# A three-layer interaction network in split precision: one 400-column matmul per chunk becomes two of 200

## The reference

```python
# x: (512, 39, 32); W0: (39*39, 200), W1 and W2: (100*39, 200)
for i in range(3):
    z = einsum('bmd,bnd->bmnd', x, hidden).reshape(B, -1, D)   # hidden = x for layer 0
    cur = relu(einsum('bcd,co->bod', z, W[i]) + b[i][None, :, None])
    if i != 2:
        hidden, direct = cur[:, :100, :], cur[:, 100:, :]
    else:
        direct = cur
    finals.append(direct)
out = concatenate(finals, axis=1).sum(axis=-1)                # (512, 400)
```

## Time and profile before

| | before |
|---|---|
| median of 3 runs | 2921.2 us (2920.04 to 2921.68) |
| the profiled execution's own time | 2919.57 us |
| its span, first to last instruction | 2917.8 us |
| mean granted clock of TensorE | 0.990 |
| busy share PE / PEld / DVE / ACT | 97% / 91% / 91% / 64% |

### The profile page before, as it was taken

How to read it: one execution, slowest core, us unless ns; L and a number is a source line. 1 busy time by engine, 2 the same in 40 slices (tenths; PEclk the granted TensorE clock), 3 DMA queues, 4 the chain that set the end, 5 groups by cost and what they waited for, 6 DMA issues and landing times.

```text
span 2917.8 us, 58694 instructions
## 1 busy us (share of the span) xinstructions
PE 2820.6 (97%) x18688; PEld 2666.4 (91%) x18688; DVE 2668.5 (91%) x2706; ACT 1873.7 (64%) x3850; POOL 1.1 (0%) x11
## 2 busy tenths in 40 slices
PE   1699999999999999999999999999999999999998
PEld 1699999999999999999999999999999999999998
DVE  3799999999999999999999999999999999999997
ACT  2466666666666666666666666666666666666665
POOL 0000000000000000000000000000000000000000
PEclk8899999999999999999999999999999999999999
DMA  8344444344444344344344344344444434444441
GB/s 193 84 130 107 107 128 110 106 127 113 104 125 117 104 124 118 104 120 121 104 118 124 104 117 125 104 112 129 104 109 128 108 107 127 111 106 126 113 106 53
DMA packets 256151, 333.83 MB, mean 114 GB/s; under 512 B 61346, under 2 KB 190990, under 8 KB 256014
## 3 DMA queue, kind: packets, MB, share of 16 engines
q1 hardware_dynamic: 256138, 333.67, 43.9%
HBM read 332.73 MB, written 8.37 MB: 117 GB/s over the span
## 4 chain that ended last, share of the span: by engine, by line
PE 95%; DMA 2%; DVE 1%; SPq 1%; ACT 1%; issue 0%; DVEq 0%; ACTq 0%
PE acc L589 62%; PE acc L590 28%; PE summed L608 4%; PE turned L601 1%; DMA xb<-x_by_unit 0%; DMA xb<-in_L_rec_b_dram 0%; DVE z_low L346 0%; DMA w_rows_again<-in_L_rec_W_dram 0%; DMA xb<-in_L_rec_W_dram 0%; DVE z L342 0%; DVE w_split L319 0%; DMA out_dram<-o_row 0%; ACT w_split L487 0%; ACT z_high L454 0%; SPq L194 0%
## 5 line engine op out<-in xcount | busy, mean ns | idle before, releaser
L589 PE MATMUL acc<-w_split,z_high 128*128 128x400 f32 (+1 forms) x8832 | 2672.9, 368 | 77.5 <-DVE z_low L346 71.6
L590 PE MATMUL acc<-w_split,z_low 128*128 128x200 f32 (+1 forms) x8832 | 2255.7, 255 | 0.0
L589 PEld LDWEIGHTS acc<-w_split,z_high 128*128 128x128 f32 (+1 forms) x8832 | 1661.5, 188 | 166.9 <-issue 159.3
L454 ACT ACTIVATE z_high<-z 128x1024 fp32r<-128x1024 f32 (+2 forms) x1152 | 1179.3, 1024 | 814.9 <-PE acc L590 737.5
L590 PEld LDWEIGHTS acc<-w_split,z_low 128*128 128x128 f32 (+1 forms) x8832 | 1690.9, 191 | 0.0
L346 DVE TENSOR_TENSOR z_low<-z,z_high 128x1024 fp32r<-128x1024 f32 (+2 forms) x1152 | 1353.4, 1175 | 129.3 <-ACT z_high L454 129.2
L342 DVE TENSOR_TENSOR z<-hid,xb 128x1024 f32<-128x1024 f32 (+1 forms) x1024 | 1213.8, 1185 | 59.7 <-DMA xb<-x_by_unit 50.9
L475 ACT ACTIVATE hid<-turned 96x512 f32<-96x512 f32 x256 | 149.1, 582 | 132.2 <-PE turned L601 132.2
L478 ACT ACTIVATE hid<-turned 32x128 f32<-32x128 f32 x768 | 204.6, 266 | 8.9
L608 PE MATMUL summed<-s,group_b 128*4 128x100 f32 (+1 forms) x768 | 150.1, 277 | 1.4 <-ACT s L470 1.4
L351 DVE TENSOR_TENSOR s<-acc,half 128x200 f32<-128x200 f32 x384 | 137.8, 359 | 10.5 <-ACT half L459 10.5
(11 more groups left out here) (20 smaller groups left out, 13.5 us busy)
## 6 DMA issues: line engine op xcount, KB each, us to landing
xb<-x_by_unit SPq DMA_DIRECT2D x384, 384.0 KB, 4.8
x_right<-x_by_unit SPq DMA_DIRECT2D x384, 136.5 KB
xb<-x_by_unit SPq DMA_DIRECT2D x384, 128.0 KB, 5.7
xb<-x_by_unit SPq DMA_DIRECT2D x128, 336.0 KB
xb<-x_by_unit SPq DMA_DIRECT2D x128, 84.0 KB
x_left<-x_by_unit SPq DMA_DIRECT2D x384, 19.5 KB
out_dram<-o_row SPq DMA_DIRECT2D x256, 1.6 KB
xb<-in_L_rec_W_dram SPq DMA_DIRECT2D x6, 600.0 KB, 9.2
```

The costliest lines, as they stand in the source:

```text
L454: nc.scalar.activation(z_high[slot][0:rows, 0:n * T], z[slot][0:rows, 0:n * T], ACT.Copy).then_inc(high, 1)
L589: nc.tensor.matmul(a[:, 0:2 * O], z_high[slot][0:rows, tok], w, start=(c == 0), stop=False, skip_group_check=True)
L590: last = nc.tensor.matmul(a[:, 0:O], z_low[slot][0:rows, tok], w[:, 0:O], start=False, stop=(c == chunks - 1), skip_group_check=True)
```

## The change

A chunk is three matmuls of 200 columns, all into the accumulator's columns 0 to 199: z_high with the high weights, z_high with the low weights, z_low with the high weights. The accumulator's second half isn't used. `half`, `second_half`, `sums`, `dup` and `relu` are gone, with their semaphores; ACT's new `outputs`, at the places of `second_half`, reads the accumulator directly: for layers 0 and 1 a copy of the 100 factors to s, the repeated tail, and the relu of the direct part; for layer 2 one relu of 200 columns. `acc_free` waits for these on ACT.

```diff
-                    nc.tensor.matmul(a[:, 0:2 * O], z_high[slot][0:rows, tok], w, start=(c == 0), stop=False, skip_group_check=True)
+                    nc.tensor.matmul(a[:, 0:O], z_high[slot][0:rows, tok], w[:, 0:O], start=(c == 0), stop=False, skip_group_check=True)
+                    nc.tensor.matmul(a[:, 0:O], z_high[slot][0:rows, tok], w[:, O:2 * O], start=False, stop=False, skip_group_check=True)
                     last = nc.tensor.matmul(a[:, 0:O], z_low[slot][0:rows, tok], w[:, 0:O], start=False, stop=(c == chunks - 1),
                                             skip_group_check=True)
...
-            def sums(l, u):
-                dve.wait_ge(half_in[l], u + 1)
-                nc.vector.tensor_tensor(s[l][:, :, 0:HID], acc[l][:, 0:O].rearrange("p (h o) -> p h o", o=HID), half[l][:, :, :], ALU.add)\
-                  .then_inc(s_in[l], 1)
...
-            def second_half(l, u, last):
+            def outputs(l, u, last):
 
                 act.wait_ge(freed, RING + last + 1)
-                nc.scalar.activation(half[l][:, :, :], acc[l][:, O:2 * O].rearrange("p (h o) -> p h o", o=HID), ACT.Copy)\
-                  .then_inc(half_in[l], 1)
...
+                if l < 2:
+                    nc.scalar.activation(s[l][:, 0, 0:HID], acc[l][:, 0:HID], ACT.Copy)
+                    nc.scalar.activation(s[l][:, 0, HID:HID + TAIL_ROWS - TAIL].rearrange("p (j q) -> p j q", q=TAIL),
+                                         acc[l][:, MAIN:HID].unsqueeze(1).to_broadcast([P, TAIL_M - 1, TAIL]), ACT.Copy)\
+                      .then_inc(factors_in[l], 1)
+                    nc.scalar.activation(s[l][:, 1, 0:HID], acc[l][:, HID:O], ACT.Relu).then_inc(direct_in[l], 1)
+                else:
+                    nc.scalar.activation(s[l][:, :, :].rearrange("p h o -> p (h o)"), acc[l][:, 0:O], ACT.Relu).then_inc(direct_in[l], 1)
...
             def acc_free(l, u):
-                pe.wait_ge(s_in[l], u)
+
+                if l < 2:
+                    pe.wait_ge(factors_in[l], u)
+                pe.wait_ge(direct_in[l], u)
```

More of the change, by code:

```diff
@@ L93, in cin_kernel @@
         s = {0: sb("s0", [P, 2, P]), 1: sb("s1", [P, 2, P]), 2: sb("s2", [P, 2, HID])}
-        half = {l: sb(f"half{l}", [P, 2, HID]) for l in range(3)}
         ident = sb("ident", [P, P])
@@ L123, in cin_kernel @@
         freed = sem("freed")
[L124 to L127, removed]
+        factors_in = [sem(f"factors_in{l}") for l in range(2)]
+        direct_in = [sem(f"direct_in{l}") for l in range(3)]
         turned_in = [sem(f"turned_in{l}") for l in range(2)]
@@ L377, in _ @@
                     lows(1, 1, L0_ROWS, L0_CHUNKS)
-                    sums(0, 0)
-                if k == 3:
-                    sums(0, 1)
             dve.wait_ge(w_low_done, 1 + 2 * GROUPS)
@@ L392, in _, with period @@
             lows(at + 4, slot_of(at + 4), L0_ROWS, L0_CHUNKS)
-            sums(1, 0)
-            sums(0, 2)
-            def period(n, par, base, sl, layer0=True, sum2=True, last_low=True):
+            def period(n, par, base, sl, layer0=True, last_low=True):
                 def slot(p):
@@ L409, in period @@
                 lows(base + 2, slot(2), P, group_chunks(2))
-                if sum2:
-                    sums(2, n - 2)
                 q = 4
@@ L425, in period @@
                 lows(base + q + 1, slot(q + 1), P, group_chunks(1))
-                sums(1, n)
                 product12(2, n - 1, 1 - par, 3, base + q + 3, slot(q + 3))
                 lows(base + q + 2, slot(q + 2), P, group_chunks(2))
-                if layer0:
-                    sums(0, n + 2)
-            period(1, 1, first(1), first(1) % RING, sum2=False, last_low=False)
+            period(1, 1, first(1), first(1) % RING, last_low=False)
             with dve.Fori(0, (UNITS - 4) // 2) as i:
@@ L440, in _ @@
             product12(2, UNITS - 1, 1, 0, at, slot_of(at))
-            sums(2, UNITS - 2)
             for g in range(1, GROUPS):
@@ L445, in _ @@
             lows(at + 3, slot_of(at + 3), P, group_chunks(3))
-            sums(2, UNITS - 1)
         @block.scalar
@@ L497, in _ @@
                     highs(1, 1, L0_ROWS, L0_CHUNKS)
[L498 to L501, removed]
+                    outputs(0, 0, 0)
                 if k == 3:
@@ L504, in _ @@
                     results(0, 0)
[L505 to L508, removed]
+                    outputs(0, 1, 1)
                 if k == 7:
@@ L516, in _ @@
             highs(at + GROUPS, slot_of(at + GROUPS), L0_ROWS, L0_CHUNKS)
[L517 to L520, removed]
+            outputs(1, 0, at + 3)
+            outputs(0, 2, at + 4)
             def period(n, par, base, sl, layer0=True, before0=True, before2=True):
@@ L527, in period @@
                 highs(base, slot(0), P, group_chunks(0))
-                if before0:
-                    dup(0, n + 1)
-                    relu(0, n + 1)
                 highs(base + 1, slot(1), P, group_chunks(1))
@@ L534, in period @@
                 if before2:
-                    second_half(2, n - 2, base - 1)
+                    outputs(2, n - 2, base - 1)
                 results(1, n - 1)
@@ L543, in period @@
                     q = 5
-                if before2:
-                    relu(2, n - 2)
                 if before0:
@@ L549, in period @@
                 highs(base + q + 1, slot(q + 1), P, group_chunks(1))
-                second_half(1, n, base + 3)
+                outputs(1, n, base + 3)
                 highs(base + q + 2, slot(q + 2), P, group_chunks(2))
                 if layer0:
-                    second_half(0, n + 2, base + 4)
+                    outputs(0, n + 2, base + 4)
                 if before2:
@@ L556, in period @@
                 highs(base + q + 3, slot(q + 3), P, group_chunks(3))
-                dup(1, n)
-                relu(1, n)
             period(1, 1, first(1), first(1) % RING, before2=False)
@@ L567, in _ @@
             hidden(1, UNITS - 1, 1)
-            second_half(2, UNITS - 2, at - 1)
+            outputs(2, UNITS - 2, at - 1)
             for g in range(GROUPS):
@@ L571, in _ @@
             results(1, UNITS - 1)
-            relu(2, UNITS - 2)
             results(2, UNITS - 2)
-            second_half(2, UNITS - 1, at + 3)
-            relu(2, UNITS - 1)
+            outputs(2, UNITS - 1, at + 3)
             results(2, UNITS - 1)
@@ L594, in acc_free @@
             def acc_free(l, u):
-                pe.wait_ge(s_in[l], u)
+                if l < 2:
+                    pe.wait_ge(factors_in[l], u)
+                pe.wait_ge(direct_in[l], u)
             def transpose(l, u):
-                pe.wait_ge(tail_dup[l], u + 1)
+                pe.wait_ge(factors_in[l], u + 1)
                 if not (isinstance(u, int) and u == 0):
@@ L603, in sum_over_d @@
             def sum_over_d(l, u):
-                pe.wait_ge(relu_done[l], u + 1)
+                pe.wait_ge(direct_in[l], u + 1)
                 if not (isinstance(u, int) and u == 0):
```

## The result

The changed kernel takes 3285.72 us (median of 4 runs, 3284.47 to 3286.97) against 2921.44 for the kernel before (2920.04 to 2922.42): 1.1247 times the time before, 95% interval 1.1228 to 1.1267, or 364 us more. The forecast was 3200, in a range of 3180 to 3290.

The account below looks back on a forecast made before the run. PE's pace after about 125 us of start bounds the kernel: 8832 chunks, each 0.0316 us longer, add 279 us to 2919.6, giving 3199; the median's 1.6 us more makes 3200 us, range 3180 to 3290.

Parts of the forecast that it names:

- What bounds the kernel: Whole kernel: about 125 us of start, then PE's pace; 1 ns per chunk is worth 8.8 us.
- Step (1): z_high matmul split in two: three load steps per chunk, 0.325 us against 0.2933, +279 us (bounds +258, +367).
- Step (2): Sums over d and transposes between groups: 1.72 us per unit remain; taken as 0, at most -10 us.
- Step (3): Copy to half and addition gone, ACT reads acc: all beside PE work, worth 0 in the steady part.
- (5): Kernel's end: about 0.7 us saved, about 1 us lost in the first chunks at lower clock; they cancel.
- Step (4): Order on ACT: a z_high conversion later by at most about 0.5 us; price 0, without cover 190 us.
- the cover: PE's two groups of 8 chunks (2.3 us each) outlast a conversion (1.0) plus a subtraction (1.2), hiding ACT's delay.
- the other signs: Profile after: 26496 loads, starts 0.11 us apart, chunk 0.325, PEld near 100%, no PE waits after 125 us, DVE 82%.
- A: Chunk matmuls: load isn't the limit, 200-column matmuls follow at 0.0933 us; chunk 0.280, about 2802 us; chance 0.06.
- B: Second z_high matmul needs no second load: chunk 0.295 us, 2920 to 2935 us; chance 0.06.
- C: PE's granted clock falls: at 1.2 GHz a chunk takes 0.63 us, time above 5500 us; chance 0.02.

Follow-up runs that it names:

- the uneven split: Kernel before with the 400-column z_high matmul split into 280 and 120 columns, copy and addition kept: 3448.48 us (ratio 1.1809).
- 64-token run: Changed kernel with the middle matmul of each chunk on 64 of 128 tokens: 3110.10 us; with the z_low matmul on 64 too: 2947.41 us.
- The runs with one part alone: Kernel before with only the z_high matmul split: 3289.36 us; changed kernel with the 400-column matmul kept, only outputs from ACT: 2916.47 us.

## Why the prediction was right, and where its size was off

**What bounds the kernel** held. The loss is PE's pace in the steady part, and from 200 to 2400 us no matmul of the changed kernel waits for data.

**Step (1), three loads, each the limit,** is the cause, and is shown from both sides: shortening the load shortens the step (3286 to 3110 to 2947), shortening the stream doesn't (19066 against 19061 matmuls), and the uneven split cost the 160 us that the sum of maxima gives. Its size was off. I took 0.1083 per step and named 0.1116 as the upper bound; measured is 0.1118 on the eleven chunks shown, and 0.1115 to 0.1117 as the mean of all such steps from 200 to 2400 us. A step of 0.112 or more was my own sign that the forecast is wrong at its upper end, and the steps stand right there. The time is in the range, with 4 us to spare, because the range was drawn from that bound and not from the value that I took. Averaged over all chunks of that stretch that follow each other directly, a chunk went from 0.2937 to 0.3346 us, 0.0409 more where I had 0.0316: 8832 x 0.0093 = 82 us, nearly all of the distance from 3200 to 3286.

The sentence that failed is "the z_low load follows a load-bound z_high matmul with no such extra". In the kernel before there are 0.0033 us from the z_low matmul's recorded start to the z_high load, and 0.1083 from there to the next load; I counted the second part alone. The 64-token run has both kinds of step side by side: 0.111 up to its short load, where the step ahead is set by a load too, and 0.108 where the step ahead is set by the stream. The uneven split has the same two values, 0.111 behind a load-bound step and 0.108 behind the one of 280 columns. So 0.108 is the price of a load step behind a stream-bound one, and between load-bound ones it is 0.003 to 0.0035 more. That this is the same 0.0033, moved, fits the sum but isn't shown. The full price could be read in the earlier trace rows by starting from a matmul whose start its stream had set: from the z_low matmul at 1004.12 to the second load behind it at 1004.24, 0.1116 on the mean of the twelve.

**Step (2), sums and transposes:** with the mean chunk, a unit has 21.96 - 69 x 0.2937 = 1.70 us beside its chunks before and 24.81 - 69 x 0.3346 = 1.72 after. The 0 that I took was right; the up to 10 us of hidden load time didn't come. (The 0.3355 of the eleven chunks shown would give 1.66, but 0.01 us of resolution over eleven chunks is 0.06 in a unit.)

**Step (3) and (5), copy, addition and end:** taken at 0, with 0.7 us saved at the end against 1 us lost in the first chunks. The runs with one part alone say 4 us for all that isn't the split. No run tells the 1 us of the first chunks apart. At the end the rows after show one relu between the last two sums:

```profile
3280.19 0.09 PEld L571 LDWEIGHTS summed<-s,group_b 128*4 128x4 f32 x2
...
3280.96 0.31 ACT L446 ACTIVATE s<-acc 128x200 f32<-128x200 f32 x1
3281.32 0.09 PEld L571 LDWEIGHTS summed<-s,group_b 128*4 128x4 f32 x2 [1.04 <-ACT s L446]
```

From sum to sum 1.13 us instead of 1.93: 0.8 us, near the expected 0.7.

**Step (4), ACT's order:** the row of matmuls has no wait for L434 or L343 from 200 to 2400 us. The row of loads has one:

```profile
PEld acc L548 <- DVE z_low L343: 45.8, 177, 0.3
```

These are the gaps around sums, which before were put down to issue (69.3 us, 301 times). They have hardly grown: a sum among chunks adds 0.534 us to the step there, and 0.528 before. So the cover held. DVE's share is the forecast 82%, but of a longer unit: 20.3 us of 24.8, where I had 19.8 of 24.1. Of the other signs, PEld near 100% didn't come: it is busy 2109 of 2200 us, 96%, since the gaps around the sums remain.

**Rivals.** A (load not the limit) is refuted by the 64-token runs and by the step itself. The prediction set beside it a formula from the Trainium skill ("TensorE: Matmul & The Clock Gate", "Back-to-back issue gap"). That section gives the formula for an isolated matmul, and says that in a stream of loads and matmuls both set the spacing, with which these runs agree (0.1115 per pair, not 0.0858). B (a second load saved) didn't happen: there are 8832 loads for the second matmul, and the order of the three makes no difference. The Trainium skill ("TensorE: Matmul & The Clock Gate", "Step-by-step: what each phase is for") is right that load and matmul are separate, but in this program each fp32r matmul brings its own load, here as before. C (the clock) did not come in the changed kernel, but it was nearer than the 0.02 suggest: with 100 columns less per chunk the same kernel ran at the lower level from start to end.

## What to carry to other kernels

Price a matmul as the longer of its stream and of the weight load that must hide behind it, and add these up one by one; splitting a wide matmul adds no columns and still costs a load step wherever the pieces are narrower than the load (here below about 240 columns, an estimate: the 0.185 us of 400 columns are 0.4625 ns per column, and 240 of them make 0.111 us). Take the step in the profile around a whole cycle, and ask of each step what set the one ahead of it, since a load step cost 0.108 behind a stream and 0.1115 behind another load. The busy share doesn't tell: it stays at 97% either way. Save engine work beside the bound last; here it was worth at most 4 us against 364.

## What was not expected of the hardware

A step set by a 128x128 fp32r load took 0.108 to 0.112 us at the full clock and 0.213 at the lower one, and a load of 64 columns brought its step down to 0.095, about the 0.093 of a 200-column stream. In two of these runs streaming less cost much more than it could have saved. With 560 instead of 600 columns per chunk and the same load-bound step, PE was still at the pace of 1.2 GHz up to 168 us, which the changed kernel had left at 121 us, ran its last 25 us at the lower clock too, and lost 35 us in all; with 500 it stayed at that pace to the end and took 6101 us. Why isn't shown. The profile's clock of 1.00 in the slow start of the one and in all of the other is contradicted by the steps: at a pace of 0.213 per load, the steps are the better witness.
